# VectorE's order in layer 0 of a three-layer graph network: edge look-ups and prefix scans later, the sums read one lot earlier

## What is computed

```
def _mean_agg(x, src, dst, n):
    msg_sum = jax.ops.segment_sum(x[src], dst, num_segments=n)
    cnt = jax.ops.segment_sum(jnp.ones((src.shape[0], 1), x.dtype), dst, num_segments=n)
    return msg_sum / jnp.maximum(cnt, 1.0)
def _sage_conv(x, src, dst, Wl, bl, Wr):
    return _mean_agg(x, src, dst, x.shape[0]) @ Wl.T + bl + x @ Wr.T
h = relu(layernorm(x))                     # 6250 x 128
h = relu(batch_norm(sage_conv(h, 128 -> 256)))
h = relu(batch_norm(sage_conv(h, 256 -> 256)))
h = sage_conv(h, 256 -> 128)
return x + log_softmax(h)
```

## Time and profile before

| | |
|---|---|
| median of three runs | 1412.6 us (1412.49 to 1419.15) |
| profiled execution, its own time | 1415.42 us |
| span in the profile | 1413.7 us |
| mean granted TensorE clock | 0.996 |
| TensorE busy, matmuls | 1329.0 us, 94% |
| VectorE busy | 582.4 us, 41% |
| ScalarE busy | 512.4 us, 36% |
| GpSimd busy | 565.5 us, 40% |

### The profile page before, as it was taken

The page is one execution under the profiler, slowest core; times in us unless marked ns, Lnnn a source line. Parts: engine busy times, 40 slices in busy tenths (PEclk is TensorE's granted clock), DMA queues, the critical chain, the costliest instruction groups (busy, mean ns, idle before and its releaser), DMA issues.

```text
span 1413.7 us, 31431 instructions
## 1 busy us (share of the span) xinstructions
PE 1329.0 (94%) x13653; PEld 835.3 (59%) x13653; DVE 582.4 (41%) x1081; ACT 512.4 (36%) x848; POOL 565.5 (40%) x562
## 2 busy tenths in 40 slices
PE   1399999999999999999999999999999999999997
PEld 0277888787778887654444444444447754444445
DVE  6988787788879832120111112011102212221223
ACT  4797879788887854410000000000000520000001
POOL 3423232424140100006576666656661026666650
PEclk9999999999999999999999999999999999999999
DMA  6155555556464551366676666666651688998983
GB/s 169 37 202 177 196 192 188 192 164 216 168 236 160 199 185 53 132 215 213 221 238 210 222 231 203 223 226 219 223 173 53 209 300 295 330 323 316 323 308 101
DMA packets 113588, 291.15 MB, mean 206 GB/s; under 512 B 19938, under 2 KB 55412, under 8 KB 113412
## 3 DMA queue, kind: packets, MB, share of 16 engines
q1 hardware_dynamic: 85196, 228.74, 46.2%
q0 software_dynamic: 21824, 55.44, 13.1%
q10 hardware_dynamic: 6424, 4.88, 1.1%
HBM read 197.78 MB, written 91.22 MB: 204 GB/s over the span
## 4 chain that ended last, share of the span: by engine, by line
PE 77%; DMA 6%; DVE 5%; issue 4%; POOL 4%; ACT 3%; DVEq 0%; ACTq 0%; SPq 0%; POOLq 0%
PE cells L1650 34%; PE bank L1223 15%; PE bank L1650 6%; PE cells L1215 5%; PE cells L1716 3%; DMA hots<-table,src_i 3%; POOL hots L548 3%; PE cells L1256 2%; DVE hots L909 2%; PE cells L1653 2%; DMA parts<-in_pairs_dram,last_i 2%; PE cells L1728 2%; PE cells L1903 1%; PE bank L1903 1%; PE bank L1229 1%
## 5 line engine op out<-in xcount | busy, mean ns | idle before, releaser
L1650 PE MATMUL cells<-ring,parts 128*128 128x500 f16 (+1 forms) x2548 | 642.1, 373 | 0.0
L548 POOL DMA_INDIRECT hots<-table,src_i x444 | 421.0, 948 | 450.4 <-DMA table<-parts 218.6
L1650 PEld LDWEIGHTS cells<-ring,parts 128*128 128x128 f16 (+1 forms) x2548 | 238.9, 96 | 284.1 <-issue 18.4
L684 ACT CAST ring<-cells 128x980 f16<-128x980 f32 (+1 forms) x325 | 330.4, 1065 | 70.2 <-PE cells L1215 68.8
L1223 PE MATMUL bank<-ring,parts 128*128 128x250 f16 (+1 forms) x2450 | 296.5, 273 | 10.5 <-DVE agm L918 9.9
L909 DVE TENSOR_TENSOR hots<-iotas,tab 128x980 f16<-128x980 f16 (+3 forms) x262 | 248.4, 1000 | 16.3 <-PE cells L1215 12.5
L1223 PEld LDWEIGHTS bank<-ring,parts 128*128 128x128 f16 (+1 forms) x2450 | 227.7, 98 | 41.1 <-issue 7.2
L1650 PE MATMUL bank<-ring,parts 128*128 128x500 f16 (+1 forms) x490 | 182.5, 372 | 0.0
L755 ACT ACTIVATE agmg<-cells,isp 128x124 f32<-128x124 f32 x16 | 5.8, 366 | 453.2 <-PE cells L1265 453.2
L1215 PE MATMUL cells<-hots 64*128 64x49 f16 x4670 | 92.5, 186 | 26.9 <-DVE hots L909 26.7
L1215 PEld LDWEIGHTS cells<-hots 64*128 64x128 f16 x4670 | 74.6, 95 | 61.2 <-DVE hots L909 31.2
(11 more groups left out here) (211 smaller groups left out, 1043.1 us busy)
## 6 DMA issues: line engine op xcount, KB each, us to landing
ring<-c_blocks SPq DMA_DIRECT2D x120, 750.0 KB, 6.5
c_blocks<-ring SPq DMA_DIRECT2D x175, 437.5 KB
ring<-c_blocks SPq DMA_DIRECT2D x40, 812.5 KB, 6.8
rcb<-rc_row SPq DMA_DIRECT2D x69, 125.0 KB
hots<-table,src_i POOLq DMA_INDIRECT x444
Z<-in_x_dram SPq DMA_DIRECT2D x4, 768.0 KB, 6.4
table<-parts SPq DMA_DIRECT2D x2, 1536.0 KB
table<-parts ACTq DMA_DIRECT2D x2, 1536.0 KB
```

The lines of the kernel that those rows point to most:

```text
L548: pool.indirect_dma_start(out=got[layer][:, 5 * (r % NGOT) + i, :], out_offset=None, in_=tables[layer], in_offset=bass.IndirectOffsetOnAxi ...
L684: act.copy(blk[c % 2][:, :, :].rearrange("p a (d g) -> p a d g", d=GD)[:, :, :, GPS * i:GPS * i + n], cells[t % NCELL][:, :, 0:n * NA].rea ...
L1650: ins = pe.matmul(bank[b][:, 0:2 * BD].rearrange("p (s d) -> p s d", s=2), lhs, ring[0:r, :, BD * a:BD * a + BD], start=(a, part) == (0, 0 ...
```

## The change

Only the order of steps changes, not an instruction. In the table of chores the batches' numbers are written out one by one. Per batch, in steps counted from the first step of the visit in which its first chores stand (visits 1, 5, 9, 13, 17):

| chore | batch 2, before | after | batches 3 to 6, before | after |
|---|---|---|---|---|
| rows | 18 | 20 | 14 | 17 |
| windows | 31 | 32 | 27 | 29 |
| firsts | 33 | 31 | 29 | 27 |
| ends | 37 | 37 | 33 | 34 |
| shifts | 40 41 42 43 | 41 42 43 44 | 36 37 38 39 | 39 41 43 44 |
| tile | 44 | 45 | 40 | 46 |
| place | 45 | 46 | 41 | 48 |
| table | 48 | 48 | 44 | 49 |
| turns | 47 49 51 55 | 47 49 51 55 | 43 45 47 55 | 45 47 50 55 |

Steps 39 to 51 are the visits 4, 8, 12, 16 and 20. In these visits VectorE's reading of the sums moves from step 4 to step 3, that is ahead of the lot of step 4 in place of behind it. Samples, reads ("row") and counts keep their steps.

```
         t0 = NST * batches[q][0]
-        scans, rows, reads, shift = ((11, 12, 14, 15), 18, (24, 25, 27, 28), 40) if q == 1 else \
-            ((2, 4, 6, 8), 14, (16, 18, 19, 21), 36)
+        scans, rows, reads, windows, firsts, ends, shifts, tile, place, table, turns = \
+            ((11, 12, 14, 15), 20, (24, 25, 27, 28), 32, 31, 37, (41, 42, 43, 44), 45, 46, 48, (47, 49, 51, 55)) if q == 1 else \
+            ((2, 4, 6, 8), 17, (16, 18, 19, 21), 29, 27, 34, (39, 41, 43, 44), 46, 48, 49, (45, 47, 50, 55))
...
-                chores[t0 + shift + k] = ("shift", q + 1, c)
-                chores[t0 + (shift + 7, shift + 9, shift + 11, 55)[k]] = ("turn", q + 1, c)
+                chores[t0 + shifts[k]] = ("shift", q + 1, c)
+                chores[t0 + turns[k]] = ("turn", q + 1, c)
...
-            chores.update({t0 + rows: ("rows", q + 1, 0), t0 + shift - 9: ("windows", q + 1, 0), t0 + shift - 7: ("firsts", q + 1, 0),
-                           t0 + shift - 3: ("ends", q + 1, 0), t0 + shift + 4: ("tile", q + 1, 0),
-                           t0 + shift + 5: ("place", q + 1, 0), t0 + shift + 8: ("table", q + 1, 0)})
+            chores.update({t0 + rows: ("rows", q + 1, 0), t0 + windows: ("windows", q + 1, 0), t0 + firsts: ("firsts", q + 1, 0),
+                           t0 + ends: ("ends", q + 1, 0), t0 + tile: ("tile", q + 1, 0), t0 + place: ("place", q + 1, 0),
+                           t0 + table: ("table", q + 1, 0)})
...
+            heads = [c0 for c0, _ in batches]
             for c in range(NB + 1):
...
-                    if c >= 2 and i == (4 if c < NB else 2):
+                    if c >= 2 and i == (2 if c == NB else 3 if c + 1 in heads else 4):
                         dve_mean(c - 2, [AGG0], 1.0 / S0, c - 1)
```

More of the change, by code:

```diff
@@ L1126, in dve_layer0 @@
                     if c == NB and i == 2:
-                        heads = [c0 for c0, _ in batches]
                         dve.wait_ge(v_count, len(batches))
```

## The result

The changed kernel takes 1434.6 us (median of four, 1433.1 to 1436.2) against 1413.8 us for the kernel before, run beside it. The recorded ratio is 1.0131, 95% interval 1.0108 to 1.0153; the two medians alone give 1.0147. It is 20.8 us slower, outside the range of 1413 to 1427. In the changed file the lines behind L80 stand one further down: L918 is L919, L1191 is L1192, L830 is L831 and so on.

A forecast was written before the change was run, and what follows sets the result against it. It took TensorE's idle time and clock to bound layer 0. Terms -8.50 - 2.85 + 8.55 + 6.18 + 4.2 + 0.7 = +8.3 us on 1412.6 gave 1420.9 us, range 1413 to 1427.

The forecast's parts named there:

- The waits at the first sums go (-8.50): TensorE's idle time before the first sums of visits 4, 8, 12, 16 and 20 disappears: -8.50 us.
- The turn waits in visits 8, 12, 16 (+8.55): TensorE's turn (L1191) waits 2.85 us for VectorE's table in each of three visits: +8.55 us.
- Visit 20 (+6.18): TensorE's turn there waits 2.85 us plus 3.33 us for the scaling of weights: +6.18 us.
- Visit 4 (0, up to 1): Table just ready for TensorE's turn in visit 4: 0, up to 1 us if the last edges land late.
- The firsts matmul: Moving TensorE's firsts matmul to an earlier step costs nothing, as it is as long there: 0.
- Late lookups (+0.7, upper bound 8.4): GpSimd's row lookups start 2.8 us later, so ScalarE may wait: +0.7 us for all, at most 8.4.
- The clock (-2.85 and +4.2, together +1.35): TensorE's two old clock losses go, -2.85 us; slow stretches follow visit 20's wait and two of three others, +4.2.
- Place excludes: Rival: VectorE's lots and GpSimd's place step exclude each other, up to 2.4 us more in four visits: 1430 us; chance 0.02.
- Faster: Rival: all five waits at the first sums go and no turn waits: 1401.3 us; chance 0.07.
- the clock stays up: Rival: TensorE's clock doesn't fall after the 2.85 us waits: 1418.1 us, or 1416.7 with visit 20 spared; chance 0.27.
- lookups late: Rival: ScalarE, and TensorE with it, waits 2.1 us for rows in each of four batches: 1428.6 us; chance 0.08.

The follow-up runs named there:

- experiment 4: Changed kernel with batches 3 to 6's shifts at 39, 41, 42, 43 and tile at 44, so place starts before a lot: 1428.8 us.
- experiment 1: Changed kernel with the reading of sums back at step 4 in visits 4, 8, 12, 16 and 20, all chores as changed: 1418.4 us.
- Experiment 8: Changed kernel with the scaling of weights moved from step 4 to 11 of visit 20, absolute weights from 10 to 12: 1428.2 us.
- Experiment 10: Changed kernel with only windows and firsts of batches 3 to 6 back at steps 27 and 29: 1429.3 us.
- Experiment 9: Changed kernel with only the rows step of batches 3 to 6 back at step 14: 1431.6 us.
- Experiments 2: Kernel before with only the reading of sums moved to step 3 in visits 4, 8, 12, 16 and 20: 1408.4 us.
- 6: Changed kernel with batches 3 to 6 reordered (early steps back, table at 46), sums read at step 3 in visit 4, step 4 elsewhere: 1404.2 us.
- 7: Kernel before with sums read at step 3 in visits 4 to 20, visit 20's scaling at step 11, absolute weights at 12: 1408.1 us.

## Why the prediction was wrong, step by step

The main step held, but not its size: the waits at the first sums went, and waits at the turn came. Three terms of the sum were too small: the clock's (+1.35 forecast, +6.25 measured), the firsts matmul's, put at nothing (3.0 measured), and the late lookups' (0.7 forecast, 2.8 measured).

**The waits at the first sums go (-8.50): right.** All five are gone.

**The turn waits in visits 8, 12, 16 (+8.55): the mechanism right, the size 10.0.** The wait was forecast at 2.85 and was 3.34 us. The step that failed was "the lots of steps 6 and 8 4.37 [...], which ran beside GpSimd's place step, as these will". They ran at 1.98 each, unhindered, and it was place that was slowed, so that VectorE waited 0.96 us for it at the table. That is 0.96 - 0.41 on the path. The other instructions came out 0.17 shorter, and TensorE was at its turn 0.1 sooner (9.4 us behind the sums' end, forecast 9.5), which makes the 0.5. In visit 20 the lots did take 4.35 us, as forecast. In experiment 4 the wait is 2.81 us. The Trainium skill (SBUF - State Buffer, "Who interferes with whom") says that the order of issue decides who is blocked; the traces agree as far as, of the 60 place steps in the twelve profiles, the 23 that began while no lot ran took 2.2 to 2.9 us, and the 37 that began 0.17 or 0.18 us behind a lot 3.45 to 3.48 (18 of them) or 7.75 to 7.77 us (19). The rival on this rule took VectorE for the loser; here the loser was GpSimd, and VectorE felt it 0.96 us later, at the table. The page also has the loser block fully. Of GpSimd that fits its first place instruction, which took 5.14 us and ended only after the second lot had; of VectorE it fits less, since a lot behind a place step lost 0.4 us, not a whole instruction. And the page does not tell why place took 3.45 us in experiment 1, where a lot was ahead of it by the same 0.17 us.

**Visit 20 (+6.18): right,** 6.13 us, and with place as forecast here (3.46 us, lots 0.4 longer). Experiment 8 shows the scaling in it.

**Visit 4 (0, up to 1): right,** 0.56 us.

**The firsts matmul ("as long at its new place: 0"): wrong, +3.0.** It isn't longer, but it stands at another step. At step 1 of a visit ScalarE is still reading the linear part out of the PSUM bank that the matmul writes (L1201 waits for L694 in four visits, and both name `bank[MISC0]` in the kernel); at step 3 it was done. I costed the move by the instruction's own time and by VectorE's gain, and did not ask who else holds its bank. Experiment 10 shows it: back at step 3 the four waits are gone.

**Late lookups (+0.7, upper bound 8.4): the mechanism right, the size about 2.8.** ScalarE waited 6.7 us in four places, 2.3 at most, against a forecast of up to 2.1 a batch, and TensorE's waits for its copies rose from 0.6 to 3.4 us. I took the low end because no such wait was in the trace before; that said nothing on how much room there was. Experiment 9 shows it: with the rows step back, TensorE's waits for the copies are 0.6 us again.

**The clock (-2.85 and +4.2, together +1.35): the largest miss, +6.25.** Three turns' waits (visits 12, 16 and 20) were followed by a half-clock stretch, as many as the forecast had; which of the three equal waits would be spared it couldn't say, and took two by choice. What it lacked is a fourth, behind the waits for ScalarE's copies in visit 14, and the price. It took each fall at 1.4 us, from waits of 2.04 and 3.05 us behind which some 3 us of work ran at the lower clock. Behind these three waits some 6 us did, which costs about 3 us each (an estimate: half of the stretch), and 3.4 us in visit 14, about 1.7. Experiments 2, 6 and 7 have no such stretch in layer 0 and a busy time of 428.9 to 429.7 us for the same matmuls; against that the stretches cost the kernel before 3.3 to 4.1 us and the changed one 9.6 to 10.4.

**The sum.** Forecast +8.3. Waits: forecast -8.50 + 8.55 + 6.18 + 0.7 = +6.9, measured +13.65, 6.7 more. Missing were 1.5 in the three turns, 3.0 in the firsts, 2.1 in the copies and 0.6 in visit 4, 7.2 in all; the other way, a wait of 0.63 us before a lot of sums at 389.22 in the trace before has no like in the changed one. Clock: +1.35 forecast, +6.25 measured. None of the rivals is what happened. "Faster" falls with the first turn that waits, "the clock stays up" with the rows at 0.51, and "lookups late" is a part of the truth at a third of its price (2.8 us of TensorE's time against 8.4). "Place excludes" is another part: the exclusion was there, but cost the path 0.55 us net in each of three visits, not 2.4 in four.

**What is open.** First, how far a single stretch at the lower clock is chance. The turn's wait of visit 8 is 3.34 us both in the changed kernel and in experiment 8. The two kernels differ in nothing before visit 20. Behind the wait the clock stayed at 1.00 in the first and fell in the second, whose busy time by stretch reads:

```profile
208.00:211.30 3.30, 3.30 (x35) 2.31 (x34) 2.43 (x4) 1.45 (x2) 0.00 (x0) 0.50 0.03 5
211.30:214.60 3.30, 3.30 (x63) 2.69 (x62) 1.56 (x2) 2.32 (x3) 0.00 (x0) 1.00 0.15 62
```

So single executions can differ by a microsecond or two for one such wait. Second, what decides between 3.45 and 7.75 us for a place step that begins 0.17 us behind a lot. In all 19 with 7.75 the lot before had ended only 0.5 us ahead of place, with two shifts between the lots; in all 18 with 3.45 it had ended 0.76 us ahead or more, with the reading of sums, the scaling or idle time in between. That was seen in the profiles but not tried as an experiment of its own, so it is not shown to be the cause. Third, the 7 us of the early steps are not divided exactly.

## What to carry to other kernels

To read a result sooner helped here only where the reading engine was late. Put ahead of work that it doesn't depend on, a wait of an engine that is early turns into idle time, and everything behind it in that engine's order is late by as much: the same edit was worth -6.2 us with one order of chores and +16.2 us with the other. In a schedule written as steps, price a move by the distance in time from the event that releases the path (here the end of the sums) to each consumer, engine by engine, and for each moved instruction list who holds its buffers at the new step, PSUM banks included. And price an idle gap of the matrix engine with its clock: here 13.65 us of added waits brought 6.25 us of slower matmuls.

## What was not expected of the hardware

Two GpSimd instructions on 128 x 256 floats took 2.90 us where they began 0.29 us before a VectorE instruction with two SBUF operands (experiment 4), and 3.45 us (experiment 1) or 7.75 us (the changed kernel) where they began 0.17 us after one. In the slow case the first of the two took 5.14 us, through two VectorE lots and the 0.42 us instruction between them, while the lots kept their 2.06 us. In the 3.45 case the cost was shared: each lot took 2.25. Why the one or the other is open.

Waits of one length, 3.34 us, were followed by no stretch at 1.2 GHz, by one of about 3 us, or by one of about 6 (visit 8 of the changed kernel, visit 8 of experiment 8, visits 12 and 16 of the changed kernel). Once the clock fell, it stayed down through 3.3 to 6.3 us of almost unbroken matmuls.
